# A graph layer on one core: x of tiles 16 to 31 loaded early, finished tiles 42 to 57 kept, ScalarE's order changed

## What is computed

```python
h = jnp.maximum(_layernorm(x, axis=-1), 0.0)
mask = adj > 0
head = mask / jnp.maximum(jnp.sqrt(jnp.sum(mask * mask, axis=-1, keepdims=True)), 1e-12)
inc = adj + head
out = x + (inc @ h) / jnp.sum(inc, axis=-1, keepdims=True)
```

## Time and profile before

| | before |
|---|---|
| median of 3 runs | 1259.71 us (1259.56 to 1262.38) |
| the profiled execution | 1265.03 us |
| its span | 1263.2 us |
| VectorE busy | 92% |
| ScalarE, TensorE matmul busy | 77%, 77% |
| GpSimd busy | 61% |
| DMA moved | 471.29 MB, 373 GB/s over the span |

### The profile page before, as it was taken

How to read it: one execution, slowest core, us unless ns; L and a number is a source line. 1 busy time by engine, 2 the same in 40 slices (tenths; PEclk the granted TensorE clock), 3 DMA queues, 4 the chain that set the end, 5 groups by cost and what they waited for, 6 DMA issues and landing times.

```text
span 1263.2 us, 14630 instructions
## 1 busy us (share of the span) xinstructions
PE 970.4 (77%) x2678; PEld 482.8 (38%) x2678; DVE 1162.8 (92%) x2794; ACT 977.8 (77%) x1903; POOL 764.9 (61%) x745
## 2 busy tenths in 40 slices
PE   0002889988888888888888888798888878878676
PEld 0001334444444434444433444344444434434343
DVE  6679999999999999999998999989999989998972
ACT  6657888898888887888887787788878778876551
POOL 1003666766666667676666666775666667667453
PEclk9999999888889999889988988988899889998698
DMA  9999999999999999999999999999999999999442
GB/s 360 428 421 406 398 402 392 392 394 399 396 391 402 401 399 398 384 401 394 384 398 368 400 398 391 388 395 373 402 400 400 385 382 387 398 399 355 142 143 79
DMA packets 148127, 471.29 MB, mean 373 GB/s; under 512 B 24386, under 2 KB 24386, under 8 KB 143876
## 3 DMA queue, kind: packets, MB, share of 16 engines
q1 hardware_dynamic: 90368, 331.38, 66.9%
q0 software_dynamic: 57664, 138.93, 29.9%
HBM read 490.21 MB, written 33.82 MB: 415 GB/s over the span
## 4 chain that ended last, share of the span: by engine, by line
DVE 45%; DMA 20%; issue 20%; ACT 5%; SPq 5%; another core or an unknown queue 2%; PE 1%; DVEq 0%; ACTq 0%; POOL 0%; POOLq 0%
DMA adj_tile<-in_adj_dram 17%; DVE folded L774 15%; DVE cand_word L779 12%; DVE cand_index L783 5%; DMA gathered_rows<-in_x_dram 3%; SPq L385 2%; ACT junk L569 2%; DVE cand_word L797 2%; SPq L392 2%; DVE cand_index L802 2%; ACT adj_tile L556 2%; SPq L396 1%; DVE ln_stats L757 1%; DVE weights_and_payload L914 1%
## 5 line engine op out<-in xcount | busy, mean ns | idle before, releaser
L488 POOL DMA_INDIRECT gathered_rows<-h_scratch,slot_column x520 | 536.8, 1032 | 265.9 <-issue 161.2
L569 ACT ACTIVATE junk<-adj_tile,zero_unit 128x2048 bf16<-128x2048 f32 x256 | 510.1, 1994 | 111.2 <-issue 75.5
L1330 PE MATMUL acc<-gathered_rows,diag 128*128 128x512 f32 x1040 | 504.1, 641 | 0.5 <-issue 0.5
L488 POOL DMA_INDIRECT gathered_rows<-h_scratch,spill_column x197 | 220.5, 1119 | 199.0 <-ACT spill_column L615 150.8
L774 DVE SCALAR_TENSOR_TENSOR folded<-adj_tile 128x1024 f32<-128x1024 f32 x248 | 301.4, 1215 | 12.1 <-DMA adj_tile<-in_adj_dram 10.7
L1330 PEld LDWEIGHTS acc<-gathered_rows,diag 128*128 128x128 f32 x1040 | 213.7, 212 | 247.1 <-issue 246.8
L779 DVE MAX8 cand_word<-folded 128x8 f32<-128x1024 f32 x248 | 302.9, 1221 | 2.2
L783 DVE FIND_INDEX8 cand_index<-cand_word,folded 128x8 uint32<-128x1024 f32 x248 | 302.2, 1218 | 0.0
L1341 PE MATMUL acc<-gathered_rows,spill_matrix 128*128 128x512 f32 x394 | 186.3, 607 | 14.6 <-issue 10.7
L632 ACT ACTIVATE diag<-ident,weights_and_payload 128x128 f32<-128x128 f32 x582 | 176.2, 387 | 0.5 <-DVE weights_and_payload L914 0.5
L1278 PE MATMUL poff<-spill_rank,lanes_before 128*128 128x1 f32 x130 | 26.4, 272 | 187.5 <-DVE spill_rank L859 174.4
(11 more groups left out here) (146 smaller groups left out, 829.8 us busy)
## 6 DMA issues: line engine op xcount, KB each, us to landing
adj_tile<-in_adj_dram SPq DMA_DIRECT2D x256, 1024.0 KB
h_scratch<-adj_tile SPq DMA_DIRECT2D x16, 1024.0 KB, 10.5
out_dram<-out_tile SPq DMA_DIRECT2D x64, 256.0 KB
gathered_rows<-in_x_dram SPq DMA_DIRECT2D x12, 1024.0 KB, 12.6
x_residual<-in_x_dram SPq DMA_DIRECT2D x48, 256.0 KB
gathered_rows<-h_scratch,slot_column POOLq DMA_INDIRECT x520
x_held<-in_x_dram SPq DMA_DIRECT2D x4, 1024.0 KB, 7.9
gathered_rows<-h_scratch,spill_column POOLq DMA_INDIRECT x197
```

The costliest lines, as they stand in the source:

```text
L488: nc.gpsimd.indirect_dma_start(out=into, out_offset=None, in_=h[:, :], in_offset=bass.IndirectOffsetOnAxis(ap=column, axis=0), bounds_chec ...
L569: nc.scalar.activation(junk[:, n % 2].rearrange("p (j c) -> p j c", j=2), both[:, :, half], ACT.Relu, bias=zero_unit[:], scale=-UP, accum_ ...
L1330: last = nc.tensor.matmul(acc[t % 3][:], diag[:, t % 2, 1 + s], slot(t % 2, s), start=False, stop=False)
```

## The change

`load_x` now takes tiles 16 to 31 into the 16 places of `held`, each as soon as the residual and the row of the tile that lies there have been made: at step t, for t from 2 to 17, x of tile t+14 is loaded, at the place in SyncE's order where x was loaded before. Tiles 32 to 63 go through `x_residual` as before, two steps ahead of their use. From step 32 on the places of `held` are idle; finished tiles 42 to 57 are copied there instead of into `out_tile`, and are not stored in steps 46 to 61 but in one block at the start of SyncE's step 62, ahead of the store of tile 58 and x of tile 62. On ScalarE, the matrices and the row of t-2 are put ahead of check 0, and check 2 is put behind the finish of t-4 and the reach of t-1.

```diff
+    KEPT = 42
...
         def x_of(t):
-            return held[:, t] if t < HELD else xres[:, t % 2]
+            return held[:, t % HELD] if t < 2 * HELD else xres[:, t % 2]
+        def kept(t):
+            return KEPT <= t < KEPT + HELD
+        def out_of(t):
+            return held[:, t - KEPT] if kept(t) else osb[:, t % 2]
+        def stored_before(t):
+            return (t if t < KEPT else t - HELD) // 2
...
             def load_x(t):
+                before = t - HELD if t < 2 * HELD else t - 2
+                if before < HELD or before >= 2 * HELD:
+                    sp.wait_ge(res_added, before + 1)
+                    if not wide(before):
+                        sp.wait_ge(row_ready, before + 1)
                 if t >= HELD + 2:
-                    sp.wait_ge(res_added, t - 1)
-                    if not wide(t - 2):
-                        sp.wait_ge(row_ready, t - 1)
-                sp.dma_start(xres[:, t % 2], x_t[t // ROWS, t % ROWS]).then_inc(x_loaded[t % 2], 16)
+                    sp.wait_ge(x_loaded[t % 2], 16 * (x_turn(t) - 1))
+                sp.dma_start(x_of(t), x_t[t // ROWS, t % ROWS]).then_inc(x_loaded[t % 2], 16)
...
                     load_chunk(t + 2, 1)
-                if t >= 4:
+                if t == KEPT + HELD + 4:
+                    for u in range(KEPT, KEPT + HELD):
+                        store_tile(u)
+                if t >= 4 and not kept(t - 4):
                     store_tile(t - 4)
-                if t >= HELD:
+                if t in range(2, HELD + 2):
+                    load_x(t + HELD - 2)
+                if t >= 2 * HELD:
                     load_x(t)
...
             def finish_tile(t):
                 act.wait_ge(acc_ready, t + 1)
-                if t >= 2:
-                    act.wait_ge(out_stored[t % 2], 16 * (t // 2))
-                nc.scalar.activation(osb[:, t % 2], acc[t % 3][:], ACT.Copy).then_inc(out_ready, 1)
+                if t >= 2 and not kept(t):
+                    act.wait_ge(out_stored[t % 2], 16 * stored_before(t))
+                nc.scalar.activation(out_of(t), acc[t % 3][:], ACT.Copy).then_inc(out_ready, 1)
...
-                check(t, 0)
                 if pay:
                     own_matrices(q)
                     if not wide(q):
                         row_again(q)
+                check(t, 0)
...
                 check(t, 1)
-                check(t, 2)
                 if end:
                     finish_tile(f)
                 if small:
                     reach_places(p)
+                check(t, 2)
                 check(t, 3)
```

More of the change, by code:

```diff
@@ L320, in add_graph_layer @@
         out_stored = [sem(f"out_stored{b}") for b in range(2)]
+        kept_stored = sem("kept_stored")
         halves_set = sem("halves_set")
@@ L387, in load_x @@
             def load_x(t):
+                before = t - HELD if t < 2 * HELD else t - 2
[3 more added lines that the diff above has]
+                        sp.wait_ge(row_ready, before + 1)
                 if t >= HELD + 2:
-                    sp.wait_ge(res_added, t - 1)
-                    if not wide(t - 2):
-                        sp.wait_ge(row_ready, t - 1)
-                sp.dma_start(xres[:, t % 2], x_t[t // ROWS, t % ROWS]).then_inc(x_loaded[t % 2], 16)
+                    sp.wait_ge(x_loaded[t % 2], 16 * (x_turn(t) - 1))
+                sp.dma_start(x_of(t), x_t[t // ROWS, t % ROWS]).then_inc(x_loaded[t % 2], 16)
             def store_tile(t):
                 sp.wait_ge(out_ready, t + 1)
-                sp.dma_start(out_t[t // ROWS, t % ROWS], osb[:, t % 2]).then_inc(out_stored[t % 2], 16)
+                sp.dma_start(out_t[t // ROWS, t % ROWS], out_of(t)).then_inc(kept_stored if kept(t) else out_stored[t % 2],
+                                                                             16)
             for c in range(4):
@@ L425, in _ @@
             for b in range(2):
-                sp.wait_ge(out_stored[b], 16 * (TILES // 2))
+                sp.wait_ge(out_stored[b], 16 * stored_before(TILES))
+            sp.wait_ge(kept_stored, 16 * HELD)
             sp.wait_ge(list_ready, 1)
@@ L536, in _ @@
             for b in range(2):
-                pool.wait_ge(out_stored[b], 16 * (TILES // 2))
+                pool.wait_ge(out_stored[b], 16 * stored_before(TILES))
+            pool.wait_ge(kept_stored, 16 * HELD)
             pool.wait_ge(out_ready, BATCH + 1)
```

## The result

| | before | after |
|---|---|---|
| median of 20 runs each | 1260.47 us (1257.73 to 1267.19) | 1257.17 us (1252.5 to 1264.89) |
| ratio, 95% interval | | 0.9971 [0.9961, 0.9981] |
| the profiled execution | 1265.03 us | 1252.5 us |
| its span | 1263.2 us | 1250.7 us |
| granted clock, mean | 0.908 | 0.917 |

The change gains 3.3 us, 0.3%, where 16 to 18 were forecast. The two profiled executions differ by 12.5 us, but that is mostly scatter: the one of after is the fastest of its 20 runs, and of the 20 runs of before only one (1267.19) is slower than its profiled one. Of the 12.5 us only 3.6 lie in the loop up to step 60; from the head of step 60 to the end the profiled execution of before takes 140.8 us and that of after 131.7, while three other kernels without kept stores (e_xearly, e_roworder, e_order) take 134.7 to 136.2 there.

The account below looks back on a forecast made before the run. VectorE's 16.685 us step plus a transfer debt was taken as the bound; loop loss 3.7 + 0.3 + 5.4 + 0.5 + 1, about 11 us, replaces 28.7, so 1243.5 us was forecast (1236 to 1248, chance 0.50), range 1236 to 1257.

Parts of the forecast that it names:

- VectorE's floor: Shortest time of a loop step, VectorE working without a gap: 16.685 us, against which losses are counted.
- debt of 0.54 us a step: Steps with both x load and store move 6.86 MB, 17.2 us, so transfers fall 0.54 us behind each step.
- the lead: Head start of the adjacency chunks, which hides the debt until about step 24: 9 x 0.54 = 4.9 us.
- thrown-away transfer time: DMA engines slow to 360 GB/s in a VectorE stall for want of freed chunks: 2.0 us lost in 21.
- `find_entry` stalls: VectorE waits for TensorE's `pbrought`, 13.0 us in 3 waits of up to 5; expected to go with ScalarE's new order.
- 16 x 0.262 = 4.19 MB leave steps 46 to 61, 10.5 us at 398 GB/s: Stores of tiles 42 to 57 leave the loop, taking 10.5 us of transfer time with them.
- Those steps are even again (6.6 MB): Without stores, steps 46 to 61 match VectorE; loss 0.5 us in 42 to 57 (0 to 2), 1 in 58 to 61.
- The early x: x loads moved to steps 2 to 17: 3.7 us lost there, 0.3 in 18 to 31, 5.4 in 32 to 41.
- Cost 0: ScalarE's matrices and row ahead of the first check cost nothing, as the check fills a 2.22 us gap.
- The block in the tail: The 16 stores at step 62 need 10.5 us and hide in 17.5 us of free DMA time: cost 0.
- no change: Rival: stalls come from TensorE's clock and stay wherever x or stores go; 1256 to 1263.5 us, chance 0.13.
- bytes only: Rival: only the 10.5 us of bytes leaving the loop are gained; 1249 us, range 1248 to 1255.9, chance 0.29.

Follow-up runs that it names:

- e_xearly: The kernel before with x of tiles 16 to 31 loaded early and nothing else: 0.9997 [0.9981, 1.0013], 1262.66 us.
- e_roworder: The kernel before with ScalarE's new order alone, but the row behind the first check: 0.9986 [0.9967, 1.0005], 1260.01 us.
- e_order: The kernel before with ScalarE's new order alone, x and stores as before: 1.0003 [0.9983, 1.0024], 1266.85 us beside 1265.21.
- e_nox: The kernel before without its 48 loads of x of tiles 16 to 63: 0.9762 [0.9738, 0.9785], 1232.46 us beside 1262.9.
- e_nostore: The kernel before without the 48 stores of tiles 16 to 63: 0.9861 [0.9832, 0.9891], 1242.23 us beside 1261.21.
- e_kept: The kernel before with tiles 42 to 57 kept and stored in one block, nothing else: 0.9956 [0.9936, 0.9976], 1259.56 us beside 1265.21.
- e_rowbehind2: The changed kernel with the row behind the first check, matrices still ahead, on a second chip: 0.992 [0.9897, 0.9943] of before, 1252.11 us.
- e_after: The changed kernel itself, run again on another chip: 0.9938 [0.9914, 0.9961] of before, 1254.28 us.
- e_after3: The changed kernel itself, run again on the chip of e_rowbehind3 and e_keptrow: 0.9947 [0.993, 0.9965] of before, 1253.81 us.
- e_keptrow: e_kept plus ScalarE's new order with the row behind the first check, so without the early x: 0.9942 [0.9926, 0.9957] of before, 1253.46 us.
- e_rowbehind3: The same kernel as e_rowbehind2 on a third chip, that of e_after3: 0.9939 [0.9916, 0.9962] of before, 1254.38 us.
- e_noblock: The changed kernel without the block of 16 stores (tiles 42 to 57 never stored): 0.9966 [0.9946, 0.9985] of before, 1256.66 us.

## Why the prediction was wrong, point by point

**The bottleneck: right.** VectorE's floor with a transfer debt on top was the reading, and taking the loads away brings the loop to that floor (e_nox) at nearly the price forecast, 0.63 us a load for 0.66. The prediction's "debt of 0.54 us a step" times 46 steps would have been 24.8 us, so part of the 30 us that came is not in it.

**"A debt of 0.54 us a step" against the 28.7 us lost: here is the largest error.** By my own price the kernel before should have lost 45 x 0.54 - 4.9 (the lead) = 19.4 us in steps 16 to 60. It lost 28.7, and I put the other 9.3 down to stalls and thrown-away transfer time, which the new order was to end, and counted them as gained. The step that failed is this one: "So I expect the `find_entry` stalls to go, and the debt to be paid in waits for chunks alone, without lost transfer time." In the form of the change the stalls shrank only (13.0 us to 2.4, 6.4 and 6.0), and e_order, with 4.0 us of them left, stands at 1.0003 [0.9983, 1.0024]. In e_roworder the stalls went and the waits stood before folds alone, and the time was 0.9986 [0.9967, 1.0005] all the same, with 31.6 us lost in the loop. So with the transfers unchanged, ending the stalls gave back nothing that can be told from zero (at most 4 us by the interval of e_roworder): a stall is a place where the debt is paid, and paid elsewhere when it is gone. Why the loss is larger than the mean bytes explain stays open.

**"16 x 0.262 = 4.19 MB leave steps 46 to 61, 10.5 us at 398 GB/s": mis-sized by nearly half.** It priced a store by its bytes at the rate of all traffic. No row showed a store's own price, and I named no bound below that. Measured, a store is worth 0.365 us (e_nostore) or 0.35 (e_kept), a load of the same bytes 0.63. Sixteen stores are worth 5.8 us, not 10.5; by the intervals, and by e_rowbehind2 beside e_roworder, 3 to 8.

**"Those steps are even again (6.6 MB)": wrong with it.** Steps 46 to 57 of after lost 9.7 us, 6.3 in e_after and 11.3 in e_after3 (forecast 0.5, at most 2, for 42 to 57). If a step without the store but with x lacked the difference of the two prices, 0.63 - 0.365 = 0.27 us, that would be 3.2 us in 12 steps. But in e_nostore the same steps carry the same traffic and lost 0.4 us. What differs is what comes before: in e_nostore no step from 20 on had a store, while after comes to step 46 from 14 steps with both transfers. So traffic that is even by its bytes does not make steps even when they start in debt; that is my reading, and no run tests it. How the 6 to 11 us come about stays open. And there was a slip: the stores that go away are those of steps 46 to 61, so steps 42 to 45 still have both transfers, 4 x 0.54 = 2.2 us that I had counted at nothing. They lost 2.7.

**The early x: right in its sum, and in two of three stages.** Steps 2 to 17 lost 4.2 us (forecast 3.7), steps 32 to 41 lost 5.5 (5.4), but steps 18 to 31 lost 3.0 (0.3, the bound was 1), and 4.4 and 3.7 in e_after and e_after3: here too steps that were to be even are not. That steps 32 to 41 came out at the forecast may be luck, since e_kept lost 2.4 there and e_keptrow 8.1. In my sum it was worth nothing by itself: the same number of full steps, the same lead spent once. e_xearly (0.9997) and e_keptrow say so too.

**"Cost 0" for ScalarE's matrices and row: incomplete.** The row ahead of the check waits for x: ScalarE stood 47 us before it in after and in e_order, and 5 us in e_keptrow, where the row is behind the check. I had weighed its wait for `weights` only. Its price in time is not settled: nothing on one chip (e_after3, e_rowbehind3), 4.6 us on another (e_noblock, e_rowbehind2).

**The block in the tail: right.** Hidden, DMA share 0.80 in 1163 to 1187 us of after (forecast near 0.7), x of tile 62 in time, and the time from the head of step 60 to the end not longer (131.7 us; 140.8 in the profiled before, 134.7 to 136.2 in other kernels without the block):

```profile
1163.00:1187.00 24.00, 14.56 (x37) 8.12 (x37) 23.41 (x53) 14.77 (x30) 10.99 (x11) 0.79 0.80 272
```

**The sum with the measured prices**: 5.8 + 0 + 0 = 6 us, 1254. Measured, by the ratios, were 3.7 in the 20 runs, 7.8 in e_after, 6.7 in e_after3. The measured 1257.17 lies in the range that I gave to "no change" (1256 to 1263.5), but the ratio is clear of 1, and its mechanism is refuted by e_nox: that the number fell there is luck. In mechanism the rival "bytes only" is the nearest (1249); with 0.365 us for a store it gives 1254. It held that late steps stay late or the lost transfer time stays, and so that no other gain comes, and no other gain was found in the change as it stands.

## What to carry to other kernels

Where VectorE's floor and the transfers are level, price a transfer by a run without it, in its own direction, before moving it: here a store was worth about 0.36 us and a load of the same size 0.63. Bytes shifted between two full stretches, or an end put to the stall in which a debt happens to be paid, gained nothing by themselves; what gained was bytes that left for a stretch with idle DMA engines. A loss larger than the mechanism explains must be left in the sum until a run shows what ends it.

## What the runs showed of the hardware

- With DMA engines busy throughout (share 1.02), a store of 0.26 MB was worth 0.365 us of the kernel's time (0.29 to 0.44 by the interval of e_nostore; 0.19 to 0.51 in e_kept) and a load of the same size 0.63 (0.57 to 0.69, e_nox). Why was not tested. The Trainium skill, page "DMA: Bandwidth & Descriptors", says under "Two DMAs through the same engine are not ordered" that an engine's read and write sides are separate queues; whether that lets a store overlap with loads in part is a guess, and no run here shows the two sides.
- Of a chunk's 16 semaphore increments, one from each DMA engine, one can come far behind others. Of the first chunk of tile 0 all 16 land within 1.3 us in before (76.2 to 77.5 us); of that of tile 10 the trace of before has six (us):

```
228.3  228.4  228.7  228.7  229.1  238.5
```

  The last is 9.4 us behind the others. e_nox has the same for this chunk (228.6 to 238.9), and there VectorE waits for no chunk at all: with chunks issued two tiles ahead, such a lag needs not cost anything. The Trainium skill, page "DMA: Bandwidth & Descriptors", Latency and other measured facts, has engines 7 and 15 usually slower. The lag agrees in kind only; which engine it was the trace does not tell, and no run ties it to the time lost.
- The length of SyncE's own issues shows the debt where the DMA share doesn't. Its issues of chunks (ns min/median/max) in steps without a debt and with one, in before, and then in e_nox:

```profile
L385 SPq DMA_DIRECT2D adj_tile<-in_adj_dram x52: 367/388/1164, 140.1 to 345.9; - x52
...
L385 SPq DMA_DIRECT2D adj_tile<-in_adj_dram x161: 367/2130/7545, 397.7 to 1097.7; - x161
...
L385 SPq DMA_DIRECT2D adj_tile<-in_adj_dram x166: 367/421/6399, 407.3 to 1096.2; - x166
```

  The DMA share is 1.02 in all three, so full DMA engines alone don't make an issue long: its median is 0.39 and 0.42 us where VectorE loses nothing and 2.13 where it does. In after the median is 1.58 us already in 130 to 350 us, where the early x is loaded.
- The scatter between runs is 2.1 us in the five runs of e_nox, 6.7 in the 19 of before on the same chip (1259.77 to 1266.42) and 12.7 on another. It does not simply go with the loss: the six runs of e_nostore lie within 15.1 us.
